# A decoder layer with experts on one core: all loads in SyncE's queue in an order of slots

## What is computed

```python
x = _layernorm(x + _L0_attn_ref(x, Wqkv, bqkv, Wo, bo))            # self attention, 16 heads of 16, causal window of 64
x = _layernorm(x + _L0_xattn_ref(x, ctx, ctx, Wq, bq, ...))        # cross attention on ctx_1024, relu on q, k, v, causal, own layernorm
x = _layernorm(x + _L0_ffn_ref(x, w_router, wi, wo))               # 8 experts, top 2, capacity 160, hidden 1024
```

```python
scores = jnp.einsum('bhid,bhjd->bhij', q, k) / sqrt(HD)
probs = jax.nn.softmax(jnp.where(mask, scores, -inf), axis=-1)
y = jnp.einsum('bhij,bhjd->bhid', probs, v)
...
expert_in = jnp.einsum('gtec,gth->egch', dispatch, x)
h = jax.nn.relu(jnp.einsum('egch,ehf->egcf', expert_in, wi))
y = jnp.einsum('gtec,egch->gth', combine, jnp.einsum('egcf,efh->egch', h, wo))
```

## Time and profile before

| engine | busy us | share of the span |
|---|---|---|
| PE (matmul) | 543.8 | 79% |
| PEld (weight load) | 421.6 | 61% |
| VectorE (DVE) | 339.0 | 49% |
| ScalarE (ACT) | 218.3 | 32% |
| GpSimd (POOL) | 147.5 | 21% |
| DMA queue q1 (SyncE's), 39.64 MB | | 35.4% of 16 engines |
| DMA queue q10 (ScalarE's), 33.21 MB | | 15.3% of 16 engines |

### The profile page before, as it was taken

The page is one execution under the profiler, slowest core; times in us unless marked ns, Lnnn a source line. Parts: engine busy times, 40 slices in busy tenths (PEclk is TensorE's granted clock), DMA queues, the critical chain, the costliest instruction groups (busy, mean ns, idle before and its releaser), DMA issues.

```text
span 690.6 us, 12843 instructions
## 1 busy us (share of the span) xinstructions
PE 543.8 (79%) x5092; PEld 421.6 (61%) x5092; DVE 339.0 (49%) x952; ACT 218.3 (32%) x491; POOL 147.5 (21%) x160
## 2 busy tenths in 40 slices
PE   5074939889898997997988668998687988998970
PEld 4052726656675765665666445777576866787860
DVE  3363615657577676776787547733333101232113
ACT  2000414354254453445445233453110100213103
POOL 4010003011021021031141650001111662322320
PEclk9577879999999999999999887999978989999995
DMA  4999654753935934935384462445555212688214
GB/s 109 202 181 131 211 85 65 96 59 63 121 45 84 113 44 74 113 47 79 48 108 72 84 160 60 152 170 178 203 180 181 62 36 58 191 251 282 32 13 131
DMA packets 56760, 78.97 MB, mean 114 GB/s; under 512 B 9294, under 2 KB 49357, under 8 KB 53628
## 3 DMA queue, kind: packets, MB, share of 16 engines
q1 hardware_dynamic: 42524, 39.64, 35.4%
q10 hardware_dynamic: 8032, 33.21, 15.3%
q0 software_dynamic: 6144, 5.29, 4.7%
HBM read 40.32 MB, written 13.74 MB: 78 GB/s over the span
## 4 chain that ended last, share of the span: by engine, by line
PE 33%; issue 8%; DVE 8%; DMA 3%; ACT 2%; SPq 1%; POOL 1%; ACTq 0%; another core or an unknown queue 0%; POOLq 0%; DVEq 0%
PE work L634 10%; PE work L648 8%; PE work L651 2%; PE work L442 2%; PE pv L560 2%; PE byk L496 1%; DVE negm L913 1%; PE work L436 1%; PE byk L492 1%; PE work L619 1%; DMA arena<-in_ffn_wi 1%; PE nat L496 1%; DVE r_c L984 1%; DVE stats_c L928 1%; PE work L599 1%
## 5 line engine op out<-in xcount | busy, mean ns | idle before, releaser
L913 DVE TENSOR_REDUCE negm<-nat 128x4 f32<-128x512 f32 (+2 forms) x192 | 120.5, 641 | 121.8 <-PE nat L496 116.6
L730 ACT ACTIVATE probs<-byk 128x512 f32<-128x512 f32 (+1 forms) x192 | 106.4, 563 | 131.1 <-PE byk L496 129.1
L496 PE MATMUL nat<-arena 96*128 96x128 bf16 (+2 forms) x512 | 74.9, 250 | 0.0
L496 PE MATMUL byk<-arena 99*128 99x128 bf16 (+2 forms) x512 | 73.1, 245 | 0.0
L1167 POOL TENSOR_TENSOR resk<-fk,parts_k 128x512 f32<-128x512 f32 x8 | 9.3, 1160 | 240.9 <-ACT fk L672 201.2
L492 PE MATMUL nat<-window_q,identb 128*128 128x384 bf16 (+1 forms) x96 | 36.5, 380 | 29.2 <-DMA arena<-parts_k 22.8
L496 PEld LDWEIGHTS nat<-arena 96*128 96x128 bf16 x512 | 47.6, 103 | 17.3 <-issue 3.9
L496 PEld LDWEIGHTS byk<-arena 99*128 99x128 bf16 x512 | 46.3, 100 | 18.6 <-issue 2.3
L492 PE MATMUL byk<-window_k,identb 128*128 128x384 bf16 (+1 forms) x96 | 34.5, 359 | 19.9 <-DMA arena<-mT 19.4
L634 PE MATMUL work<-woT,arena 128*128 128x160 f32 x256 | 46.5, 341 | 4.2 <-issue 4.0
L634 PE MATMUL work<-yn_T,arena 128*128 128x160 f32 x256 | 40.6, 313 | 10.6 <-DMA arena<-in_ffn_wi 6.0
(11 more groups left out here) (189 smaller groups left out, 951.5 us busy)
## 6 DMA issues: line engine op xcount, KB each, us to landing
arena<-parts_q SPq DMA_DIRECT2D x96, 128.0 KB, 5.0
arena<-parts_k SPq DMA_DIRECT2D x96, 128.0 KB, 5.3
...
token_y<-xres SPq DMA_DIRECT2D x8, 256.0 KB, 2.2
```

The source lines that it names most:

```text
L496: last = nc.tensor.matmul(bank[:, i * w:(i + 1) * w], lhsT, rhs, start=False, stop=(i == heads - 1), skip_group_check=True)
L730: nc.scalar.activation(dst, src, ACT.Exp, scale=0.25).then_inc(exp_ready, 1)
L913: V.tensor_reduce(dst, src, AX, ALU.max, negate=True).then_inc(nat_free[job % 2], 1)
```

## The change

SyncE issues all loads. `LOADS` is now a list of 13 slots for SyncE's handler LD. The first weights are cut in two: those of q, then x of batch 0 and the biases, then those of k, then x of batch 1. The rows (biases and norms) come as one row for v of the self attention, early, and the other four at slot 15. The four pieces of ones come together at slot -9.8. x of batches 2 and 3 comes at slots -4 and 8. The residual x comes batch by batch (XL), 256 KB at slot 9 of each self unit, under two semaphores in turn. The clear of `x_dram` is 13 DMAs of 200 KB (CL) at slots 44 to 104, from a piece of fq that batch 3 writes, so QC waits for them at batch 3. PE waits for the identity at its first N job instead of at its start, and VectorE's two memsets of the v tiles move to other slots.

```diff
-LOADS = ((-20, 0), (-17.3, 1), (-16, 2), (-5, 3), (-4, 4), (2, 5), (6, 6), (14, 7), (22, 8), (26, 9))
+LOADS = (-10, -9.9, -9.8, -4, 8, 15, 15.1, 19, 19.1, 28, 32, 40, 50)
+CLEARS, FILL = 13, 400
...
+            add(n0 + 9, "XL", k)
...
-    for at, i in LOADS:
+    for i, at in enumerate(LOADS):
         add(at, "LD", i)
+    for i in range(CLEARS):
+        add(44 + 5 * i, "CL", i)
...
-        no_rows = flat(fq, "s c t")[:, X1S * C * T - 4 * ROW:]
+        no_rows = fq[:, GB - 1, :, :].rearrange("p c t -> p (c t)")[:, 0:FILL]
...
-            sp.dma_start(ws[:, :, 0:2 * D], a["w_s_qk"]).then_inc(ws_in, 16)
-
+            sp.dma_start(ws[:, :, 0:D], a["w_s_qk"][:, :, 0:D]).then_inc(ws_in[0], 16)
             sp.dma_start(xT[:, 0, :, :], a["x_T"][0]).then_inc(x_in[0], 16)
             sp.dma_start(bias[:, :], a["bias"]).then_inc(bias_in, 16)
+            sp.dma_start(ws[:, :, D:2 * D], a["w_s_qk"][:, :, D:2 * D]).then_inc(ws_in[1], 16)
+            sp.dma_start(x_T(1), a["x_T"][1]).then_inc(x_in[1], 16)
+
+            def LD(i, n, layer, b):
+
+                if i == 0:
+                    sp.dma_start(ws[:, :, 2 * D:3 * D], a["w_s_v"]).then_inc(w_s_v_in, 16)
+                elif i == 1:
+                    sp.dma_start(rows[:, 0:1, :], a["rows"][0:1, :].partition_broadcast(P)).then_inc(bv_in, 16)
+                elif i == 2:
+                    sp.wait_ge(pool_cols, 1)
+                    ones_rows = arena[KR:KR + MR, :].bitcast(BF16).rearrange("p (i n a b) -> p i n a b", i=PAIRS, n=2, b=P)[:, :, 1, :, :]
+                    for pair in range(PAIRS):
+                        sp.dma_start(ones_rows[:, pair, :, :], onesb[0:MR, :].unsqueeze(1).broadcast_to([MR, H * T // P, P]))\
+                            .then_inc(ones_in, 16)
+                elif i == 3:
+                    sp.dma_start(x_T(2), a["x_T"][2]).then_inc(x_in[2], 16)
+                elif i == 4:
+                    sp.dma_start(x_T(3), a["x_T"][3]).then_inc(x_in[3], 16)
+                elif i == 5:
+                    sp.dma_start(rows[:, 1:5, :], a["rows"][1:5, :].partition_broadcast(P)).then_inc(rows_in, 16)
+                elif i == 6:
+                    sp.dma_start(woT[:, :, :], a["w_s_o"]).then_inc(w_s_o_in, 16)
+                elif i == 7:
+                    sp.dma_start(wc["k"][:, :, :], a["w_c_k"]).then_inc(wc_in["k"], 16)
+                elif i == 8:
+                    sp.dma_start(cT[:, 0, :, :], a["ctx_T"][0]).then_inc(c_in[0], 16)
+                elif i == 9:
+                    sp.dma_start(wc["q"][:, :, :], a["w_c_q"]).then_inc(wc_in["q"], 16)
+                elif i == 10:
+                    sp.dma_start(cT[:, 1, :, :], a["ctx_T"][1]).then_inc(c_in[1], 16)
+                elif i == 11:
+                    sp.dma_start(wc["v"][:, :, :], a["w_c_v"]).then_inc(wc_in["v"], 16)
+                else:
+                    sp.dma_start(wr[:, :, :], a["w_router"]).then_inc(wr_in, 16)
+
+            def XL(k, n, layer, b):
+                wait(sp, xb_ready, b - 1)
+                sp.dma_start(xres[:, b * QT:(b + 1) * QT, 0:D], a["x"][b].rearrange("(t p) d -> p t d", p=P)).then_inc(xres_in[b % 2], 16)
+
+            def CL(i, n, layer, b):
+
+                if i == 0:
+                    sp.wait_ge(zeros_ready, 1)
+                sp.dma_start(x_dram.rearrange("(p n) d -> p (n d)", p=P)[:, i * FILL:(i + 1) * FILL], no_rows).then_inc(cleared, 16)
...
-                if k < PAIRS:
-                    if k == 0:
-                        sp.wait_ge(pool_cols, 1)
-                    sp.dma_start(stack["k", k][KR:KR + MR, :, :].rearrange("p h t -> p (h t)").rearrange("p (a b) -> p a b", b=P),
-                                 onesb[0:MR, :].unsqueeze(1).broadcast_to([MR, H * T // P, P])).then_inc(ones_in[k], 16)
 
...
-                    pe.wait_ge(ws_in, 16)
+                    pe.wait_ge(ws_in[0], 16)
...
             def KS(k, n, layer, b):
+                if b == 0:
+                    pe.wait_ge(ws_in[1], 16)
...
+                        pe.wait_ge(ident_ready, 1)
...
-                    if k < PAIRS:
-                        pe.wait_ge(ones_in[k], 16)
+                    if k == 0:
+                        pe.wait_ge(ones_in, 16 * PAIRS)
...
-                elif b == 1:
-                    act.wait_ge(cleared, 16)
+                elif b == GB - 1:
+                    act.wait_ge(cleared, 16 * CLEARS)
...
-            def LD(i, n, layer, b):
-
-                if i == 0:
-                    nc.scalar.dma_start(x_T(1), a["x_T"][1]).then_inc(x_in[1], 16)
...
-                    nc.scalar.dma_start(xres[:, :, 0:D], a["x"].rearrange("b (t p) d -> p (b t) d", p=P)).then_inc(xres_in, 16)
...
-            def clear(k, n, layer, b):
-                if b == 0:
-                    act.wait_ge(zeros_ready, 1)
-                    nc.scalar.dma_start(x_dram.rearrange("(p n a) d -> p n (a d)", p=P, a=4),
-                                        no_rows.unsqueeze(1).broadcast_to([P, E * GROUPS * CAP // P // 4, 4 * ROW])).then_inc(cleared, 16)
 
...
-                if i in (2, 3):
-                    link(V.memset(vone["sc"[i - 2]][:, :, :, :, :], 1.0))
+                if i in (0, 3):
+                    link(V.memset(vone["s" if i == 0 else "c"][:, :, :, :, :], 1.0))
...
-                    dve.wait_ge(rows_in, 16)
+                    dve.wait_ge(bv_in if layer == "s" else rows_in, 16)
...
-                if b == 0:
-                    pool.wait_ge(xres_in, 16)
+                pool.wait_ge(xres_in[b % 2], 16 * (b // 2 + 1))
...
-                        pool.wait_ge(cleared, 16)
+                        pool.wait_ge(cleared, 16 * CLEARS)
```

More of the change, by code:

```diff
@@ L273, in attention_and_experts @@
         y_dram = nc.dram_tensor("token_y", [TOKENS + P + P // 4, D], F32).ap()
-        ws_in = sem("ws_in"); bias_in = sem("bias_in"); w_s_v_in = sem("w_s_v_in"); rows_in = sem("rows_in"); w_s_o_in = sem("w_s_o_in")
-        wc_in = {n: sem(f"w_c_{n}_in") for n in "qkv"}; wr_in = sem("wr_in"); xres_in = sem("xres_in")
+        ws_in = sems("ws_in", 2); bias_in = sem("bias_in"); w_s_v_in = sem("w_s_v_in"); bv_in = sem("bv_in"); rows_in = sem("rows_in"); w_s_o_in = sem("w_s_o_in")
+        wc_in = {n: sem(f"w_c_{n}_in") for n in "qkv"}; wr_in = sem("wr_in"); xres_in = sems("xres_in", 2)
         x_in = sems("x_in", TOK + 1); c_in = sems("c_in", TOK)
         cleared = sem("cleared"); zeros_ready = sem("zeros_ready")
-        ident_ready = sem("ident_ready"); masks_ready = sem("masks_ready"); pool_consts = sem("pool_consts"); ones_in = sems("ones_in", PAIRS)
+        ident_ready = sem("ident_ready"); masks_ready = sem("masks_ready"); pool_consts = sem("pool_consts"); ones_in = sem("ones_in")
         v_ones = sem("v_ones"); eps_ready = sem("eps_ready")
@@ L422, in FS @@
                 sp.dma_start(out_v[:, b * QT:(b + 1) * QT, :], xres[:, b * QT:(b + 1) * QT, 0:D]).then_inc(out_stored, 16)
-            walk({"LX": LX, "LC": LC, "SQ": side_q, "SC": side_q, "SK": side_k, "CK": side_k, "MT": MT, "EL": EL, "XS": XS, "FL": FL, "FS": FS})
+            walk({"LD": LD, "XL": XL, "CL": CL, "LX": LX, "LC": LC, "SQ": side_q, "SC": side_q, "SK": side_k, "CK": side_k, "MT": MT, "EL": EL, "XS": XS, "FL": FL, "FS": FS})
             sp.wait_ge(out_stored, 16 * B)
@@ L655, in EY @@
                 work_job("EY", x, emit)
-            pe.wait_ge(ident_ready, 1)
             walk({"QS": QS, "KS": KS, "VS": VS, "KC": KC, "VC": VC, "XC": XC, "QC": QC, "N": N, "MT": MT, "T": T_, "PV": PV,
@@ L760, in GC @@
                 nc.scalar.activation(expd[:, n * GT:(n + 1) * GT, :], diff[:, n * GT:(n + 1) * GT, :], ACT.Exp).then_inc(expd_ready, 1)
-            def LD(i, n, layer, b):
-                if i == 0:
-                    nc.scalar.dma_start(x_T(1), a["x_T"][1]).then_inc(x_in[1], 16)
-                elif i == 1:
-                    nc.scalar.dma_start(x_T(2), a["x_T"][2]).then_inc(x_in[2], 16)
-                    nc.scalar.dma_start(ws[:, :, 2 * D:3 * D], a["w_s_v"]).then_inc(w_s_v_in, 16)
-                elif i == 2:
-                    nc.scalar.dma_start(rows[:, :, :], a["rows"].partition_broadcast(P)).then_inc(rows_in, 16)
-                    nc.scalar.dma_start(x_T(3), a["x_T"][3]).then_inc(x_in[3], 16)
-                elif i == 3:
-                    nc.scalar.dma_start(xres[:, :, 0:D], a["x"].rearrange("b (t p) d -> p (b t) d", p=P)).then_inc(xres_in, 16)
-                elif i == 4:
-                    nc.scalar.dma_start(woT[:, :, :], a["w_s_o"]).then_inc(w_s_o_in, 16)
-                elif i == 5:
-                    nc.scalar.dma_start(wc["k"][:, :, :], a["w_c_k"]).then_inc(wc_in["k"], 16)
-                elif i == 6:
-                    nc.scalar.dma_start(cT[:, 0, :, :], a["ctx_T"][0]).then_inc(c_in[0], 16)
-                elif i == 7:
-                    nc.scalar.dma_start(wc["q"][:, :, :], a["w_c_q"]).then_inc(wc_in["q"], 16)
-                elif i == 8:
```

(6 more changed lines are left out.)

## The result

The changed kernel takes 695.06 us (median of 20 runs, 689.56 to 698.14) against 690.18 us (20 runs) of the kernel before, measured beside it: the ratio is 1.0063 with the interval [1.0039, 1.0087]. It is slower by 0.6%, a change that the interval tells from none. The prediction said 683 us, a gain, with 677 to 692 as its range. Single executions now and then are slower throughout (911.33 us once among the 20 of the kernel before), and the ratios leave these out. The profiled execution took 695.47 us, its span is 693.6 us, and the mean granted clock of PE is 0.902 where it was 0.909.

What follows compares the result with a forecast made beforehand. PE's early stalls for k stacks and mT, caused by queueing, were taken as the bound; 692.64 - 14.0 (gained at T(1)) + 5.0 (lost in the steady stretch) = 683.6 us, 683 as a median, range 677 to 692.

Steps and rivals of the forecast that it cites:

- N(0): Start of unit 0's first N job on PE, after its k stack landed; predicted at 24.0 us instead of 35.89.
- QS of unit 2: PE job after six N jobs, needing x of batch 2; predicted to start at 37.6 us instead of 40.75.
- T(1): Start of unit 1's first T job, waiting for mT; predicted at 82.8 us instead of 96.84, 14.0 earlier.
- T(3): Start of a later T job; mT behind two clears and one piece of x, 2.2 us plus 1 for clock lost.
- the new wait: PE waiting at QS of unit 2 for x of batch 2 behind unit 1's stacks; leaves 3.1 of 12 us gained.
- the ones: Four DMAs issued by SyncE before q1's stack, reckoned at 4 x 0.89 us, putting that stack's issue at 24.3.
- the slow rival: Stacks move at 121 GB/s from the start; 7.7 us gained, 5.0 lost, 689 us as a median; chance 0.18.
- T(0): Start of unit 0's first T job, after mT and unit 3's QS; predicted at 60.2 us instead of 69.35.
- The steady stretch: After T(1), clears and pieces of x queue ahead of mT; predicted 5.0 us lost, bounds 1 and 15.
- the slower rival: Clears and pieces of x move at 121 GB/s, losing 15 us at three mT waits; from 694 us, chance 0.10.

## Why the prediction was wrong

**What held.** The first matmul (4.75, predicted 4.5); that unit 0's stack had been slowed by the 2 MB load (with x in one load again N(0) is 5.4 us later), and that PE's idleness would move to QS of unit 2; that what T(1) gains, the end gains, on the whole; that giving up ScalarE's queue costs no bandwidth (119 GB/s from two queues); that clears do not hold up mT (1.26 us of wait at T(3), 1.31 before).

**The step that failed is the stacks' rate in the part on N(0) and the new wait:** "13.3 + 10.6 = 23.9" and "so it moves from 26.3 to 36.9", both at 149 GB/s. Measured, 118 to 121 in the four windows with stacks alone. The 149 was the mean of five microseconds of a trace in which the earlier trace rows had 121 for seven. The prediction held the 149 against the rival with 121, and gave that 0.18. It tied the rate to what the compute engines do, and read the 149 as with PE half busy; that row has PE busy for 4.85 of the 5 us. It had 179 with all engines idle, and in the window from 33 to 40 us, with all of them idle, it was 119. With 118 GB/s the prediction's own sum gives N(0) at 26.6 instead of 24.0, of the 27.15 measured, and QS of unit 2 at 41.9.

**The second failed term is the ones,** reckoned as 3.6 us of issue, then 24.3 as the issue of q1's stack. That was 4 times the issue of one such DMA, 0.89 us. Between stacks they took 5.26 us to issue (q1's stack at 26.04) and left the tail in which the DMA engines stand at 0.19 while PE waits; moved to the front they gave back 4.7 us at QS of unit 2, the faster stacks of that run included. QS came 4.3 us later even than the slow rival's 41.5, and T(0) at 72.32 instead of its 66.5. Of 9.15 us predicted at T(0), none was left.

**From QS of unit 2 to T(0)** 22.6 us were reckoned and it took 26.5. The rate makes 2.7 of the 3.9 (q2's stack issued at 52.70, QS of unit 3 at 68.74: 16.0 us for 13.3). Most of the rest is the low clock: the two QS jobs took 3.74 and 3.78 us, where the prediction had 2.80 for each from the trace before, at a granted clock of 0.50.

**T(0) to T(1)** was reckoned at 22.6 us at the steady rate and took 24.2; the 1.5 us more lie behind the issue of q3's stack (20.0 us to T(1), reckoned 18.2). So of the predicted gain of 14.0 us at T(1) 0.4 remained: the slow rival had 7.7, the ones take 4.6 of it by their own run, and the low clock and the stretch before T(1) are of the size of the other 2.7, though no run takes them apart.

**The steady stretch** was predicted at 5.0 us lost, for the wrong reason. The wait for mT at T(3) is 1.26 us where 3.5 was expected, and without the clears the total is the same within the intervals. The total, 0.6% or 4 to 5 us above before with no gain at T(1), says that about as much as predicted is lost behind T(1); the traces show 2.8 of it up to T(12), against a scatter of 3 us for one kernel. Of that, 0.7 is the addition that now collides with the cast. The prediction had used that same interference for q's cast and did not ask where the later additions would land. The granted clock in 200 to 300 us is 0.95 instead of 0.97, with the waits of PE from 100 to 300 us the same list but for 0.7 us until the cast's result; but the version with x of batch 2 early had 0.98 and 0.95 in two executions. So the 5.0 is right in size by luck, and the cause of most of the loss stays open. That cutting up the clear alone cost nothing behind T(1) (0.9957 at 94.23) points away from the clears; the pieces of x and the order of the other loads were not tested apart.

**The number** fell where the slower rival had it (from 694, at 0.10), but not by its mechanism: that had the clears and pieces of x cost 15 us at three waits for mT. Of the signs of being wrong, QS of unit 2 later than 41 came, at 45.78; the wait at T(1) stayed under 9 (8.68), and no series of waits for mT came.

Stays open: what sets the rate of a stack. In the kernel before, the row with 149 is sound (from 56 to 61 us SyncE's queue moved 0.74 of 0.75 MB, 813 of 814 packets under 2 KB, while a load waited in ScalarE's), and so is the one with 179. From 47 to 52 us, in contrast, a third of the 145 GB/s were loads of ScalarE's queue. No experiment told why the same copies then move at 118 to 121 in most traces and at 125 to 133 with the ones first; the load of x in one piece did not bring the higher rate back (123).
